# Attention in pairs of steps: one stay on TensorE's column tiles, or two with maxima between them

## The reference

```python
x = x + 0.5 * ffn(layernorm(x))          # T = 2 x 2048 tokens, width 512
x = x + attention(layernorm(x))          # 16 heads of 32
x = x + 0.5 * ffn(layernorm(x))

# attention, per batch of 2048 tokens and per head
scores = Q @ K.T / sqrt(32)              # causal: only keys up to the query
A  = softmax(scores)                     # exp(s - row maximum) / row sum
AV = A @ V
return AV @ Wo + bo
```

## Time and profile before

| | |
|---|---|
| median of 3 runs | 2852.85 us (2834.76 to 2857.68) |
| profiled execution | 2841.95 us, its span 2840.2 us |
| TensorE busy | 2652.5 us, 93% |
| VectorE busy | 1991.2 us, 70% |
| GpSimd busy | 1563.5 us, 55% |
| ScalarE busy | 1477.1 us, 52% |
| chain that ended last | TensorE 64%, VectorE 17%, GpSimd 5%, ScalarE 4% |
| attention of batch 0, of batch 1 | about 851 to 1413 us, and 1619 to 2181 us |

### The profile page before, as it was taken

How to read it: one execution, slowest core, us unless ns; L and a number is a source line. 1 busy time by engine, 2 the same in 40 slices (tenths; PEclk the granted TensorE clock), 3 DMA queues, 4 the chain that set the end, 5 groups by cost and what they waited for, 6 DMA issues and landing times.

```text
span 2840.2 us, 39556 instructions
## 1 busy us (share of the span) xinstructions
PE 2652.5 (93%) x14559; PEld 1662.1 (59%) x14559; DVE 1991.2 (70%) x3565; ACT 1477.1 (52%) x2791; POOL 1563.5 (55%) x1079
## 2 busy tenths in 40 slices
PE   5799999997998999999899999999999899999997
PEld 4678888875773333333377633333334688888886
DVE  8877777777758777776197587777762777777764
ACT  4466666654213565656522145656555356666664
POOL 5556666664222566655632135666557356666665
PEclk9999999998999999999999999999999999999999
DMA  2002311122022020200140310202002501111101
GB/s 60 15 31 112 134 45 38 45 75 74 30 52 57 5 47 5 62 5 3 35 160 30 82 28 5 47 6 62 4 4 109 218 16 45 45 45 45 45 30 45
DMA packets 75712, 142.10 MB, mean 50 GB/s; under 512 B 18783, under 2 KB 22394, under 8 KB 75390
## 3 DMA queue, kind: packets, MB, share of 16 engines
q1 hardware_dynamic: 75518, 139.58, 15.6%
HBM read 74.00 MB, written 37.22 MB: 39 GB/s over the span
## 4 chain that ended last, share of the span: by engine, by line
PE 64%; DVE 17%; POOL 5%; ACT 4%; issue 3%; DMA 2%; SPq 1%; POOLq 0%; DVEq 0%; ACTq 0%
PE pp L94 48%; PE ps L94 15%; DVE sb L115 6%; POOL sb L103 5%; ACT sb L100 4%; DVE sb L109 3%; DVE sb L103 2%; DVE sb L106 2%; SPq L136 1%; DVE sb L121 1%; DVE sb L112 1%; PE ps L97 1%; DMA sb<-xa 1%; DMA sb<-xc 0%; DVE sb L124 0%
## 5 line engine op out<-in xcount | busy, mean ns | idle before, releaser
L103 POOL TENSOR_TENSOR sb<-sb,sb 128x512 f32<-128x512 f32 (+5 forms) x1062 | 1555.9, 1486 | 1273.4 <-PE pp L94 495.7
L94 PE MATMUL pp<-sb,sb 128*128 128x512 f32 (+9 forms) x11154 | 2173.2, 433 | 68.3 <-DVE sb L109 17.4
L94 PEld LDWEIGHTS pp<-sb,sb 128*128 128x128 f32 (+4 forms) x11154 | 1229.6, 143 | 796.5 <-issue 324.2
L100 ACT ACTIVATE sb<-pp 128x512 f32<-128x512 f32 (+4 forms) x1434 | 680.9, 549 | 522.5 <-PE pp L94 501.5
L94 PE MATMUL ps<-sb,sb 128*128 128x512 f32 (+5 forms) x2862 | 768.3, 358 | 67.8 <-DVE sb L115 25.1
L115 DVE TENSOR_REDUCE sb<-ps 128x1 f32<-128x512 f32 (+3 forms) x754 | 480.7, 670 | 138.2 <-PE ps L94 136.4
L100 ACT ACTIVATE sb<-sb 128x512 f32<-128x512 f32 (+3 forms) x468 | 301.5, 649 | 513.6 <-DVE sb L109 385.8
L94 PEld LDWEIGHTS ps<-sb,sb 128*128 128x128 f32 (+3 forms) x2862 | 387.4, 147 | 303.2 <-DVE sb L115 137.0
L109 DVE SCALAR_TENSOR_TENSOR sb<-ps,sb,sb 128x512 f32<-128x512 f32 x437 | 318.7, 747 | 126.1 <-PE ps L94 103.7
L109 DVE SCALAR_TENSOR_TENSOR sb<-pp,sb,sb 128x512 f32<-128x512 f32 x443 | 321.5, 745 | 117.7 <-PE pp L94 112.9
L115 DVE TENSOR_REDUCE sb<-pp 128x1 f32<-128x512 f32 (+2 forms) x366 | 243.0, 664 | 102.7 <-PE pp L94 101.5
(11 more groups left out here) (23 smaller groups left out, 395.3 us busy)
## 6 DMA issues: line engine op xcount, KB each, us to landing
sb<-sb SPq DMA_DIRECT2D x192, 128.0 KB, 2.4
sb<-L_attn_X SPq DMA_DIRECT2D x64, 256.0 KB, 3.4
sb<-xa SPq DMA_DIRECT2D x64, 256.0 KB, 5.2
sb<-xc SPq DMA_DIRECT2D x64, 256.0 KB, 3.5
xa<-sb SPq DMA_DIRECT2D x32, 256.0 KB, 2.0
xc<-sb SPq DMA_DIRECT2D x32, 256.0 KB, 6.2
out<-sb SPq DMA_DIRECT2D x32, 256.0 KB, 2.0
dg<-sb SPq DMA_DIRECT2D x11, 512.0 KB, 6.1
```

The costliest lines, as they stand in the source:

```text
L94: return self.e.matmul(*a, **k) if self.e else self
L100: return self.e.activation(*a, **k) if self.e else self
L103: return self.e.tensor_tensor(*a, **k) if self.e else self
```

## The change

The 8 calls after the scores now count 1.75 instead of 2.5 for each query column, and a new call, with 6 for each column of step m, stands between total and the second weigh. For a pair of full steps the sum is the same (8 x 2.5 = 8 x 1.75 + 6 = 20). What that call emits, maxima and one event from `parts`, lies between two stays of 8 and of 4 column-tile matmuls.

```diff
@@ Att.order
                 for j in range(4):
                     out.append(("score", n, j))
-                    advance(2.5 * (512 - offset(n)))
+                    advance(1.75 * (512 - offset(n)))
...
             out.append(("weigh", m))
             if m:
                 self.sum_up(out, parts, m - 1)
+            advance(6 * (512 - offset(m)))
             out.append(("weigh", m + 1))
```

## The result

The changed kernel took 2866.11 us (median of 8 runs, 2855.72 to 2871.62), the kernel before 2850.84 beside it (8 runs, 2834.76 to 2857.68). The ratio is 1.0062 [1.0035, 1.0089]: slower by 0.6%, which is real and within 1%. The forecast was 2857, within 1%, and the range held the time. By the profiled executions it is 2862.12 against 2841.95, where the forecast for this was 2847.

What follows compares the result with a forecast made beforehand. TensorE was taken as the bound, with ScalarE setting a 6.06 us floor per pair. Terms +7 and -5 a batch, times two, gave +4 or 5 us: 2847 profiled, 2857 against the runs' median; range 2818 to 2892.

Steps and rivals of the forecast that it cites:

- Second stay, 0.22: TensorE's two array switches per extra stay cost 0.22 us, unhidden; 69 of them make 15 us a batch.
- The higher price of 0.35: Alternative cost of a stay on TensorE, from the skill's drain of about 175 ns; sum 18 us higher.
- The units: Maxima moved into gaps change pair beats: 9 units -0.25, 8 +0.2, 6 or 7 +0.35, short +0.5; +10 us a batch.
- the guess on which the first two terms rest: Stretch of scores with 6 units: pair takes 6.06 + 0.25 us, between bounds 6.06 and 6.82.
- Pairs 1 to 3, -3: VectorE-bound early pairs gain 1 us each as gap units fill its idle time; -3 us a batch.
- The combines, -5 a batch: Combines meeting GpSimd additions: old clashes go, four new ones cost +4.6; whole -5 us a batch.
- What was to go, 9.4: Clashes in pairs 15 and 35 vanish, -7.4 us a batch, and milder ones in pairs 55 and 62, -2.
- The rest at nothing: Inversion step, `wo_split`, `av_split`, second weigh, row copies and pairs 70 to 79 change by 0.
- The waits: VectorE's wait behind a stay well under 2.06 us; TensorE's waits for VectorE mostly gone, for ScalarE grown.
- the rival of combines in the gap: Four gap combines cost 3.7 us each, as pair 15's did; 2883 us with early pairs giving nothing; chance 0.08.
- TensorE did not wait in the gap: Judges the rival that gap units lack free banks and delay the second weigh, 0.3 us a gap, 2898; chance 0.09.
- The floor was reached: Rival: 5 or 6 units hide wholly behind ScalarE and stalls vanish, giving 2815 us; chance 0.13.

Runs made afterwards that it cites:

- e1: Kernel before, plus a one-column full-array matmul between total and second weigh of pairs 0 to 68; 2877.59 us, ratio 1.0088 to the kernel before.
- e10: Kernel before with combines held back, splits at the batch's end, and gaps in 31 full pairs a batch; 2825.21 us, ratio 0.9899 to before.
- e2: Changed kernel with combines from pair 4 on held until score 5 or 6, rows 3 units later; 2853.45 us, ratio 1.0004 to before.
- e5: Kernel before with combines held until score 5 or 6, rows 3 units later; 2831.58 us, ratio 0.9944 to before.
- e6: Kernel before with combines held back and splits moved behind the last scores of pairs 71 to 78; 2813.69 us, ratio 0.9882 to before.

## Why the prediction was right, and which step was mis-sized

The total lies within 9 us of the median, and the parts act as they were described. But the change itself was forecast at +4 or 5 us and is +15 by the medians, and a wide range, 2818 to 2892, helped to hold it. The gain was put too high in one place, the combines, and the cost of the units too low.

- **Second stay, 0.22: right.** 0.24 in the trace and 0.25 by e1, its column included. "Nothing hides it" holds but for pairs 21, 41, 61 and 68. The higher price of 0.35 falls.
- **The units: right in sign in every class, low in sum.** Predicted -0.25, +0.2, +0.35, +0.5; measured -0.25, +0.37, +0.30, +0.53 where no combine or split stands in the beat, and +0.73 over all short pairs. For the stretch of scores with 6 units, the guess on which the first two terms rest, 6.31 was forecast and 6.29 measured (e10). For 9 units 7.2 was forecast, and 6.97 to 7.36 measured. With 6 or 7 two errors cancelled: I had the new beat too high (6.95, measured 6.3 to 6.6), and set it against 6.6, the beat behind a full total, where the beats of full pairs in this class all hold a short one (5.98 to 6.17). Short pairs added most: their beats held 1 to 4 units and now hold 2 to 5, those of the full gap ahead among them, which I priced as "1 or 2 units, little saved". It could have been read from the order.
- **Pairs 1 to 3, -3: wrong,** +1.8 and +0.3. Pair 2 became 2.69 shorter, but pair 1 took 2.40 longer and pair 3 2.09 (0.59 in batch 1). The order tells much of it: the gaps moved units between these beats, which hold 14, 23 and 23 where they held 10, 27 and 21, two more in all, and VectorE needs 0.6 us for each. Pair 3 also takes different times with the same order (17.14 and 16.23 us in the two batches of e2).
- **The combines, -5 a batch: the step that failed, in size.** I priced those in the gap at 1, 0.5, 2.5 and 0.6 us for pairs 9, 10, 14 and 49. Against e2 they cost 4.5, nothing, 3.9 and 1.4. The rule I had given, that a cast is caught if it starts after the addition, was right; that the one of pair 9 would start in time was a guess, and it missed by 0.08 us. What was to go, 9.4, was 7.6 and 8.4 (e5). A clash in pairs 15 and 35 was priced at 3.7, over a beat of 7.45; these beats hold 8 units, which take 6.82, so it costs 4.3 and 4.2, of which some 1.4 is the lower clock behind it (by e1). So combines made the change +2.7 and +1.7 a batch, where I had -5. That is the rival of combines in the gap, in part.
- **The rest at nothing: right.** The tail is unchanged to 0.01 us a pair, and `wo_split` kept its clash (pair 53, 13.18 to 12.94).
- **The waits: half right.** Waits for VectorE fell and those for ScalarE rose, as said; but VectorE's idle time behind a stay was only cut in two.

The rivals: TensorE did not wait in the gap. From pair 4 on no wait over 0.15 us stands in one; those of the combines (1.98 and 1.57) and of `wo_split` (3.38) come behind the second stay. The floor was reached, as the waits for ScalarE show, but this gave nothing back.

The larger terms of this kernel lay where the change did not act: combines and splits that meet GpSimd's additions cost at least 20 us a batch (e6, which still has four casts beside additions), more than the change moved.

Open: why the short pairs 11 and 51, with 5 units, take 5.93 and 5.85 in e2, where pairs 19 and 39, also with 5, take 5.11 and 5.22; why pair 3 differs with the same order; and the price of the two switches apart from e1's one column.

## What to carry to other kernels

Moving work out of a stretch that waits for engine A pays only until engine B's chain sets it; read B's time per iteration first, and count the price of the new place in every iteration, those too that had no wait. Where one list sets the order, each edit slides all rare events behind it: list them, and ask for each, before and after, which long instruction of another engine it meets, with the start times beside each other, since 0.08 us decided 4.5 us here. Where such a clash makes TensorE stand, read its granted clock behind the wait too. Such events may be worth more than the edit itself.

## What the runs showed of the hardware

- A VectorE cast of 128x16 takes 0.175 us, and 2.30 when it starts just behind a GpSimd addition of 2.35; it ends with the addition. Reductions beside the same additions are not slowed (1.28 for two of 128x512, in the earlier trace rows and in the gap).
- Such a clash costs a pair about twice its wait: TensorE stood 1.98 us, the pair took 4.5 longer, and its mean granted clock fell from 1.00 to 0.86. The clock is a part of it by itself: in pair 15 the same clash took 11.16 us with a wait of 1.88 and a mean clock of 0.85, and 9.52 us with a wait of 1.63 and a clock of 1.00 (e1).
- A matmul of one column on the full array costs 0.25 us when it stands between column-tile matmuls (e1), more than one of 512 columns among its like (0.22).
